# The first experts' activation: one ScalarE function against a ScalarE tanh and a VectorE product

## The reference

```python
gating = softmax(X @ Wg + bg)            # 8 experts, the best 2 of each token are used
h1 = einsum('bsd,edh->bseh', X, W1) + b1 # hidden size 256
h3 = einsum('bsd,edh->bseh', X, W3) + b3
h  = silu(h1 * h3)                       # silu(z) = z * sigmoid(z)
expert_outputs = einsum('bseh,eho->bseo', h, W2) + b2
mixed = sum of the two chosen outputs by their gating weights
return mixed @ Wf + bf
```

## Time and profile before

| | |
|---|---|
| runs | 1479.24, 1481.67, 1487.11 us; median 1481.67 us |
| profiled execution | span 1476.7 us from first to last instruction; no other time of it is given |
| fastest run less the span | 2.5 us, what lies around the span |
| busy share | PE 92%, PEld 81%, DVE 76%, POOL 58%, ACT 54% |
| chain that ended last | PE 63%, DVE 15%, POOL 9%, issue 7%, ACT 3% |
| expert stage | first up0 at 240.32 us, last down0 ends at about 359.2 us |
| granted TensorE clock | 0.988 of full speed over the span, 1.00 in the expert stage |

### The profile page before, as it was taken

One profiled execution on the slowest core, in us unless ns is written; L12 is line 12 of the kernel. 1 busy time (PEld: TensorE's weight loads), 2 busy tenths in 40 slices (PEclk: granted clock), 3 DMA queues, 4 the chain that ended last, 5 costly groups with the idle time before them and its releaser, 6 DMA issues.

```text
span 1476.7 us, 32500 instructions
## 1 busy us (share of the span) xinstructions
PE 1359.3 (92%) x10047; PEld 1189.8 (81%) x10047; DVE 1117.9 (76%) x3711; ACT 800.0 (54%) x1719; POOL 857.3 (58%) x1694
## 2 busy tenths in 40 slices
PE   5999998998899899999999999999999999899964
PEld 5558897886788789889888988988998889788842
DVE  7828785997788688788878878886887878554765
ACT  3646664444566566656666665665666566432321
POOL 5248783444776665745655574565557576633552
PEclk9999999999999999999999999999999999999997
DMA  7026002423300000000000000000000000012221
GB/s 250 12 82 210 25 23 86 121 73 99 98 19 3 18 16 9 18 12 9 9 14 16 8 17 11 10 7 16 16 9 10 19 11 5 12 51 76 64 82 41
DMA packets 70106, 62.25 MB, mean 42 GB/s; under 512 B 10808, under 2 KB 58019, under 8 KB 69938
## 3 DMA queue, kind: packets, MB, share of 16 engines
q1 hardware_dynamic: 61746, 44.96, 10.1%
q0 software_dynamic: 8192, 15.23, 3.5%
HBM read 32.88 MB, written 25.17 MB: 39 GB/s over the span
## 4 chain that ended last, share of the span: by engine, by line
PE 63%; DVE 15%; POOL 9%; issue 7%; ACT 3%; POOLq 2%; DVEq 1%; DMA 1%; SPq 0%
PE sa L1875 13%; PE sc L1853 11%; PE mb L1882 10%; PE tr L1864 7%; PE sc L1712 4%; DVE kept L1391 4%; POOL attn L790 3%; DVE top L1381 3%; PE mb L2091 2%; PE sc L1812 2%; PE sc L1855 2%; POOL x_slots L759 1%; PE sc L2079 1%; PE tr L1717 1%; PE sa L1919 1%
## 5 line engine op out<-in xcount | busy, mean ns | idle before, releaser
L790 POOL TENSOR_SCALAR attn<-kept,rden 128x128 f32<-128x128 f32 (+3 forms) x512 | 290.4, 567 | 340.3 <-DVE rden L1395 287.2
L1381 DVE MAX8 top<-sc 128x8 f32<-128x144 f32 (+3 forms) x512 | 263.2, 514 | 152.4 <-PE sc L1855 151.8
L1853 PE MATMUL sc<-k_hl,x_hl 128*128 128x272 f32 (+3 forms) x1920 | 370.0, 312 | 3.2 <-DVE k_hl L1373 1.7
L1875 PE MATMUL sa<-wv,attnT 128*128 128x128 f32 x2560 | 371.9, 276 | 0.0
L1021 ACT ACTIVATE attnT<-tr 128x128 f32<-128x128 f32 (+3 forms) x512 | 224.0, 437 | 269.2 <-PE tr L1864 257.5
L1875 PEld LDWEIGHTS sa<-wv,attnT 128*128 128x128 f32 x2560 | 327.7, 192 | 6.1 <-issue 6.1
L1015 ACT ACTIVATE ex<-sc,nmax 128x144 f32<-128x144 f32 (+3 forms) x512 | 277.5, 542 | 100.7 <-DVE nmax L1383 94.0
L1853 PEld LDWEIGHTS sc<-k_hl,x_hl 128*128 128x128 f32 x1920 | 280.9, 190 | 22.7 <-issue 12.4
L1391 DVE SCALAR_TENSOR_TENSOR kept<-sc,top,ex 128x144 f32<-128x144 f32 (+3 forms) x512 | 289.5, 565 | 0.6 <-issue 0.6
L1864 PE MATMUL tr<-ident,attn 128*128 128x128 f32 x1280 | 231.0, 279 | 42.4 <-POOL attn L790 40.2
L1864 PEld LDWEIGHTS tr<-ident,attn 128*128 128x128 f32 x1280 | 139.0, 142 | 56.0 <-POOL attn L790 51.6
(11 more groups left out here) (331 smaller groups left out, 1950.4 us busy)
## 6 DMA issues: line engine op xcount, KB each, us to landing
x_slots<-sg SPq DMA_DIRECT2D x1, 4608.0 KB, 17.0
y_slots<-wv SPq DMA_DIRECT2D x18, 256.0 KB, 2.3
x_slots<-sg SPq DMA_DIRECT2D x1, 2560.0 KB
y_pick<-x_slots SPq DMA_DIRECT2D x10, 256.0 KB, 2.8
fb<-L_ffn_b SPq DMA_DIRECT2D x2, 1024.0 KB, 9.6
attn<-x_slots SPq DMA_DIRECT2D x8, 256.0 KB, 3.4
arena<-L_attn_x SPq DMA_DIRECT2D x8, 256.0 KB, 3.1
fb<-L_ffn_W SPq DMA_DIRECT2D x8, 256.0 KB, 6.3
```

The costliest lines, as they stand in the source:

```text
L790: pool.tensor_scalar(dst, src[:, NM:NM + P * (t + 1)], rden[:, t:t + 1], 1.0, ALU.mult, ALU.mult).then_inc(attn_ready.sem, 1)
L1381: dve.max(top8[:, t, :], src).then_inc(top_done.sem, 1)
L1853: pe.matmul(dst[:, lo:hi], x_hl[:, a, t * P:(t + 1) * P], k_hl[:, m, k, lo:hi], start=(i == 0), stop=(i == 2 and hi < w), skip_group_check ...
L1875: ins = pe.matmul(sa[:, t * C:(t + 1) * C], src[:, j * P:(j + 1) * P], wv[:, j, k, :], start=False, stop=False, skip_group_check=True)
```

## The change

In `tanh0`, now called `silu0` on ScalarE, the function Tanh with scale 0.5 becomes Silu with no scale, and it signals `hh0_ready` itself. VectorE's `silu0`, its 36 calls and the semaphore `th0_ready` go. The scale 0.5 goes from the four copies that write `w2f`. The order of everything else is as it was.

```diff
-            def tanh0(d):
+            def silu0(d):
                 act.wait_ge(hu0_ready, d + 1)
                 if d >= 2:
                     act.wait_ge(hh0T_ps, d - 1)
-                act.activation(hh0[d % 2], hu0[d % 2], ACT.Tanh, scale=0.5).then_inc(th0_ready, 1)
+                act.activation(hh0[d % 2], hu0[d % 2], ACT.Silu).then_inc(hh0_ready, 1)
...
-            copied(w2f[:, 0:2, :, :].rearrange("p e m c -> p (e m c)"), mb[:, :], 4, scale=0.5)
+            copied(w2f[:, 0:2, :, :].rearrange("p e m c -> p (e m c)"), mb[:, :], 4)
...
                 if 1 <= d <= DUOS0:
-                    tanh0(d - 1)
+                    silu0(d - 1)
...
-            def silu0(d):
-                dve.wait_ge(th0_ready, d + 1)
-                dve.scalar_tensor_tensor(out=hh0[d % 2], in0=hh0[d % 2], scalar=1.0, in1=hu0[d % 2],
-                                         op0=ALU.add, op1=ALU.mult).then_inc(hh0_ready, 1)
...
                 if d + 1 < DUOS0:
                     load_experts(d + 1)
-                if 1 <= d <= DUOS0:
-                    silu0(d - 1)
```

More of the change, by code:

```diff
@@ L327, in build @@
         hu0_ready = sem("hu0_ready")
-        th0_ready = sem("th0_ready")
         hh0_ready = sem("hh0_ready")
@@ L1104, in _ @@
             next(rest)
-            copied(w2f[:, 0:2, :, :].rearrange("p e m c -> p (e m c)"), mb[:, :], 4, scale=0.5)
-            copied(w2f[:, 2:4, :, :].rearrange("p e m c -> p (e m c)"), bank(2), 5, scale=0.5)
+            copied(w2f[:, 0:2, :, :].rearrange("p e m c -> p (e m c)"), mb[:, :], 4)
+            copied(w2f[:, 2:4, :, :].rearrange("p e m c -> p (e m c)"), bank(2), 5)
             next(rest)
-            copied(w2f[:, 4:6, :, :].rearrange("p e m c -> p (e m c)"), bank(3), 6, scale=0.5)
+            copied(w2f[:, 4:6, :, :].rearrange("p e m c -> p (e m c)"), bank(3), 6)
             high0(0)
-            copied(w2f[:, 6:8, :, :].rearrange("p e m c -> p (e m c)"), bank(4), 7, scale=0.5)
+            copied(w2f[:, 6:8, :, :].rearrange("p e m c -> p (e m c)"), bank(4), 7)
             for q in range(2):
```

## The result

| | before | changed |
|---|---|---|
| median of 6 runs each | 1480.66 us (1478.62 to 1487.4) | 1472.28 us (1468.63 to 1476.34) |
| span of the profiled execution | 1476.7 us | 1474.6 us, that run took 1476.34 us |
| ratio | | 0.993, 95% interval 0.9909 to 0.9951 |
| first `up0` to first exp of batch 1 | 123.0 us | 114.9 us |

What follows compares the result with a forecast made beforehand. TensorE, busy 92% of the span, was taken to bound the kernel, so only its standstill could be won. Steady, first and last turns gave 6.4 + 1.0 + 1.1 = 8.5 us, from 1481.67 to 1473.2 us, range 1469 to 1481.

Steps and rivals of the forecast that it cites:

- Steady turns: Middle of the expert stage: TensorE sets the pace and each of 16 stalls of 0.40 us goes, gain 6.4 us.
- What was late, and why: Odd turns: VectorE's product of 1.34 us was late, a stall of 0.40 us before TensorE's transposes of `hh`.
- The slack: Steady turns: the new chain to `hh` takes 3.6 to 4.0 us of 5.97 us, leaving 2.0 us.
- rival B: Another queue, likeliest ScalarE's, holds TensorE in odd turns; 1476.4 us with half of each stall left, 1479.6 with all; chance 0.20.
- First turns: Start of the expert stage: the first transposes of `hh` come earlier, gain 1.0 us, bounds 0.8 and 1.1.
- Last turns: End of the stage: bias additions start earlier (0.72), GpSimd's product shortens (0.36), gain 1.1 us, bounds 0.7 and 2.0.
- Table loads: Two added loads before the first new activation and the first exp of batch 1, hidden in ScalarE's idle time, cost 0.
- rival D: New function's table lacks plain copies, so ScalarE loads four times a period; stage grows 30 us, to 1511; chance 0.04.
- The sum: Gains of steady, first and last turns: 6.4 + 1.0 + 1.1 = 8.5 us, giving 1473.2 us.
- The signs: Wrong if the period stayed above 6.1, more than three loads stood, or stage shrank 8 us and span much less.
- A: The change does what was forecast: 1473.2 us, own range 1470 to 1476, chance 0.58.
- C: Loads exposed or batch 1's start set by another release: 1.3 to 4 us come back, 1474.5 to 1477; chance 0.15.

Runs made afterwards that it cites:

- experiment 1: Changed kernel with Tanh (scale 0.5) in Silu's place, still no product on VectorE: 1472.0 us against 1480.89, ratio 0.9955.
- Experiment 3: Changed kernel with VectorE's product put back in its old place behind the same wait, on buffers of its own: 1480.29 us against 1480.89, ratio 1.0003.
- experiment 4: Changed kernel with VectorE's idle product on its own buffers, without the wait for ScalarE: 1473.37 us against 1480.89, ratio 0.9961.
- Experiments 5 and 6: Kernel before, VectorE's product kept but moved behind low part and finished group's additions: 1484.44 us; moved behind the low part only: 1481.6 us.
- experiment 8: Changed kernel with first low part and expert-number reads earlier, and duo 34 evicted ahead of duo 35's activation: 1469.67 us against 1480.97, ratio 0.9916.

## Why the prediction was right, point by point

- **Steady turns.** The step held: TensorE sets the pace, and every stall went. Its size was low: 6.37 - 5.88 = 0.49 us a period where 0.40 was taken, so 7.8 us for 16 periods and not 6.4 (from the first transposes of `hh` to the last `up0` it is 101.9 us before and 94.2 in experiment 1). The 0.40 is there (1.87 to 1.47). The rest is in what follows a stall. The transposes after it took 0.50 us to the next group before (287.81 to 288.31 in the trace) and take 0.43 now (284.01 to 284.44). The bound of 0.45 per stall, 7.2 us, stands in no row shown and was too low also. VectorE's work in a period fell to 61.48 / 90 x 5.88 = 4.0 us, not 3.74.
- **What was late, and why.** Here the reasoning was incomplete. I named the product of 1.34 us in TensorE's chain. Experiment 3 shows that the period stays at 6.3 with the product out of that chain, as long as it waits in VectorE's queue; experiment 4 shows that without the wait it is 6.03, so the rest down to 5.88 is VectorE's load. Experiments 5 and 6 show that taking the wait from in front of the low part gains nothing while the product stays in the chain. The change gained because it removes both at once. The sentence that VectorE no longer holds back the bias additions behind a product was the one that carried the gain, and the sum did not rest on it: that the stall of TensorE gave nearly the right size is in part luck.
- **The slack** of the new chain was put at 2.0 us. An activation at 287.86 ends at 288.48 and is used at 289.89: 1.4 us. What was missed is that it queues behind the eviction of `tr` on ScalarE: GpSimd's product has ended at 286.98, 0.88 us before. The room is also smaller than the 5.97 us stated, since that runs from the start of `up0`; from its end at 284.17 to 289.89 it is 5.7. It is the queue of rival B, with slack left.
- **First turns.** From the first `up0` to the first transposes of `hh` 7.30 us before. With TensorE at full clock it is 6.35 in experiment 3 (240.71 to 247.06), 6.34 in experiment 8 and 6.32 in experiment 1, so at least 0.95 for the 1.0 forecast.
- **Last turns.** The last activation comes 4.47 us after the start of the last `up0` instead of 5.57, and the last eviction 6.65 instead of 7.76: 1.1 us each, as forecast, from the bias additions and from GpSimd's product. The bias additions start 1.80 us after the last `up0` (2.53 before). GpSimd's product takes 1.295 and 1.298 us on the mean in the two buffers, where it took 1.656 and 1.292. The Trainium skill (SBUF — State Buffer, Who interferes with whom) says that a VectorE instruction with two SBUF inputs contends with a GpSimd instruction that reads SBUF; these numbers agree with it. The first exp comes another 0.35 us sooner (12.35 against 13.80), which was not forecast.
- **Table loads.** Three in all, at 0.79, 248.62 and 356.87; neither of the two new ones is on the path (experiment 1). The Trainium skill's price of a load (ScalarE: Activation LUTs, What ACT_TABLE_LOAD costs) agrees with the 1283 ns of the rows; its drain of some 1380 ns shows in no run here, with 36 added loads in one of them. The Trainium skill's statement that copies are in every set (the same page, Table sets) agrees with the trace too: evictions by copy stand between the activations of the changed kernel without a load, so rival D was nowhere.
- **The sum.** By the trace at full clock it is 7.8 + 0.95 + 1.45 = 10.2 us. Before and experiment 1, both at full clock up to 1,280 us, differ by 9.7 in their spans. So the forecast of 8.5 was 1.7 too low for the stage, 1.4 of which is the steady term. The stage in the two profiles shrank by 8.1, as that of the changed kernel had lost 2.1 us to the clock, and the medians shrank by 8.4 and 7.9. That they hit 8.5 so closely is in part luck. The clock may be what makes up the difference, but two variants of the kernel before (experiments 5 and 6) lost clock at the same place, so how often either kernel does is not known.
- **The signs.** One sign of being wrong did appear, a stage that shrinks by 8 us and a span by much less (2.1 us). It came from which two executions were profiled, as told in the first section, not from work that moved behind the stage. A slip in the chances: the rest of A, B and C adds to 0.41 and slower to 0.07, not 0.42 and 0.06.

## What to carry to other kernels

When an engine that is not the bottleneck both waits and works in the middle of its queue, look for a closed loop: add up one round from an instruction over the other engines back to the same instruction of the next round. If the sum is the period and no instruction of the loop waits for the bottleneck, that loop sets the pace, and the row that the bottleneck waits for is only where it shows. Here it was better to remove the instruction that waits in the middle of such a queue than to move it within the queue, because what the wait had covered (register reads of about half a microsecond) then stood in the chain. A table load cost nothing here where ScalarE would wait anyway. Where a single-buffered eviction stood behind it, two loads of 1.28 us made a period 0.7 us longer, though ScalarE's work fitted.

## What the runs showed of the hardware

TensorE's clock at the start of the stage. In both profiles of the changed kernel the first group of six matmuls took 2.92 us instead of 1.65, after TensorE had stood still for 2.87 us. In both the granted clock was 0.50 from 244 to 246 us and from 247 to 250, which is the level of 1.2 GHz in place of 2.4, and 1.00 between 255 and 345. Wider windows of the first of them, from 240 to 246 and from 246 to 255, hold both levels (the clock is the third number from the end):

```profile
240.00:246.00 6.00, 3.13 (x15) 2.68 (x15) 1.51 (x4) 2.53 (x6) 0.00 (x0) 0.79 0.30 87
246.00:255.00 9.00, 8.56 (x37) 6.72 (x36) 5.92 (x10) 4.30 (x7) 3.85 (x3) 0.76 0.37 105
```

Of 11 profiles 5 have a clock under 1.00 between 236 and 256 us. Ten had stood still for 2.87 to 2.97 us ahead of the first `up0`, and five of those kept the clock, so the idle time alone does not decide it; the one with 1.35 (experiment 8) kept it too, which one profile cannot prove. It costs 7.95 - 6.35 = 1.6 us up to the first transposes of `hh`, and 0.5 more up to the second (2.44 us later instead of 1.95). The granted clock over the whole span also goes with the time of a run: of six runs of the changed kernel the fastest, 1468.63 us, had 0.990 and the slowest, 1476.34, had 0.983. So part of the scatter of 0.5% that makes this change hard to measure goes with the clock; no run varied the clock alone.
